# The end of a decoder kernel: seventeen stages over four token tiles, in one order for every engine

## The chip, the cores and the metric

The kernel runs on one core of one Trainium2 chip. The metric is the time of one execution on the device, in microseconds (us); the median of three runs of the kernel before is 2982.27 us (2980.43 to 2983.85). One further execution was profiled; all rows below are from it.

## The reference

2048 tokens (32 sequences of 64) of 512 features pass through three residual blocks, each on a layer-normalised input:

```python
x = x + mamba(_layernorm(x))        # in_proj, causal conv of 4 taps, silu, chunked scan with 128 heads,
                                    # gate, RMS norm over 8 groups of 1024, out_proj
x = x + attention(_layernorm(x), ctx, ctx, mask)   # 32 query heads of 16, 8 key/value heads, over 64 context rows
x = x + lora_moe(_layernorm(x))     # 4 experts of rank 16, top 2, softmax gates
```

In the attention, per sequence: `scores = q k / 4 + mask`, `probs = softmax(scores)`, `out = probs v`. In the last block: `logits = x Wr`, the two largest of four are kept and go through a softmax, `mid = x A`, `delta = sum over experts of gate * (mid B)`. The change leaves all of this as it is. The RMS norm divides each group's output by the root of its mean square; its sum of squares over the 8 chunks of a group is what the first moved piece of work computes.

## The kernel before

**The loop.** The tokens are cut into 4 blocks (`tb`) of 512, and the first block of layers into 8 groups (`g`); that gives 32 iterations (`ITERS`) of `body(tb, g)`. One iteration has 8 chunks (`CPG`). For each chunk TensorE computes the projections (`unit`, 12 matmuls of 128x512), the scan (`heads`) and the output projection (`project`, 12 matmuls into the four banks `p_out[0..3]`, one for each of the block's four tiles of 128 tokens). VectorE does the convolution, the gating (`gated`) and the sums; ScalarE the silu, the squares (`square`) and the copies `g_hi`; GpSimd the remainders `g_lo` (`g_low`), the running sum of squares (`sum_squares`) and the decays. The order of each engine's instructions is written out by hand in its own block of the program, and the engines meet only in semaphores. Weights come from rings in SBUF (`w_ring`, `o_ring`) that the SyncE queue refills.

**The tiles in the loop.** The attention and the expert layer of a finished tile of 128 tokens are spread over the next block's iterations: tile `t` opens in an even `g` (`opening`) and closes in the odd one after it (`closing`), in slots between the chunks, in the buffers `loop_tile`. 12 tiles go that way (`LOOP_TILES`). In the closing iteration GpSimd subtracts the maxima (`shifted`), ScalarE takes the exponential (`soft_exp`); VectorE has found the maxima at the end of the opening one (`maxima`).

**The end of the last iteration.** After the loop TensorE does `heads(6)`, `project(5)`, `project(6)`, `mean_squares` (4 matmuls of the summed squares `ss` with a column of ones, which the trace shows as 8 instructions) and `project(7)`. GpSimd adds the last two chunks' squares to `ss` before it makes the last remainder, so `mean_squares` waits for ScalarE and for two additions on GpSimd. VectorE then runs `accumulate`: once all four `p_out` banks are done (`out_done`), it adds them, times the inverse root `rms`, to the four tiles in `acb`, one after the other (line 1217), and counts `acc_done` once.

**The tail.** Then follow the attention and the experts of the last four tiles (`q` 0 to 3, buffers `tail_tiles[q]`) and the last five stages of tile 11, which the loop has left (`LATE`). One tile has 14 stages:

- 0: moments (VectorE, lines 1275 to 1277) and inverse deviation (GpSimd, line 1512)
- 1: the context transposed, keys and values masked (GpSimd, lines 1519 and 1521), the row normalised (`query`, line 1282), transposed (line 582) and copied to SBUF
- 2, 3: scores of each half of the heads (16 matmul instructions each) and their scaling with the mask (`scored`, line 1289)
- 4: maxima (line 1296) and their subtraction (GpSimd, line 1527), over all 2048 columns; 5: exponential
- 6, 7: sums and reciprocals (lines 1301 and 1302), probabilities transposed by halves (line 609, 8 instructions each) and copied
- 8: values (64 matmul instructions), `attended` (line 1308), `residual` (line 1319) with moments
- 9: `expert_row` (line 1326), transposed (line 628) and copied; 10: `low_rank`
- 11: `logits` and `experts` (lines 1332 to 1352); 12: `gated`, a transpose; 13: `delta` (2 matmul instructions of 512 columns) and `result` (line 1359). The tile's store follows.

`waves(stage)` sets the order, the same on each engine: wave `w` issues stage `w - q` of tile `q`, so each tile is one whole stage behind the one ahead of it, and 17 waves make up the tail. Each engine takes its instructions strictly in this order; one that waits holds up all behind it. The tiles' PSUM banks are `p_in` (q 0), `p_out[0], p_out[1]` (q 1), `p_out[2], p_out[3]` (q 2) and `p_y` (q 3). The four tiles' contexts are loaded once the last `project` is done. In SBUF, `tail_tiles` lie over the buffers of the loop.

## Time and profile before

| | us |
|---|---|
| median of 3 runs | 2982.27 |
| lowest and highest | 2980.43, 2983.85 |
| the profiled execution | 2982.17 |
| its span, first to last instruction | 2980.4 |
| last matmul of the loop's own iterations ends | 2867.15 |
| first accumulate (line 1217) starts | 2880.59 |
| last result (line 1359) ends | 2977.92 |

The span ends with the landing of the last store. "Idle before" in a row is the time for which the engine had nothing to do ahead of that group, and the name behind the arrow is what it waited for. PEclk is the granted TensorE clock as a share of its full 2.4 GHz; it stands at one of two levels, 1.00 (2.4 GHz) or 0.50 (1.2 GHz), and a value between them is a stretch that holds both. In a timeline, a group's duration covers all its instructions, and the next group's start may lie a little before its end. All numbers in these rows are of the one profiled execution.

### The profile page before, as it was taken

Reading aid. Unit: us, or ns where it says so; the run is one execution under the profiler, and the core shown is the slowest. Engines: PE = TensorE matmul, PEld = TensorE weight load, DVE = VectorE, ACT = ScalarE, POOL = GpSimd, SP = SyncE. Lnnn points to the kernel's source line nnn. Section 1 sums busy time; section 2 is a strip of 40 time slices with the busy share of each in tenths; the row PEclk is TensorE's granted clock in tenths of the full one; section 3 lists DMA queues with packets and bytes.
Section 4 is the critical chain, followed back from the end, with each engine's and each line's share of the span. In section 5 each row is a group of like instructions: output and inputs, shape, how many; then the busy total and the mean of one; then the engine's idle time right before and its main releaser. Section 6 shows DMA issues by size and latency. Waiting matters only on the chain.

```text
span 2980.4 us, 56255 instructions
## 1 busy us (share of the span) xinstructions
PE 2861.6 (96%) x22224; PEld 2292.7 (77%) x22224; DVE 2031.6 (68%) x3144; ACT 1454.3 (49%) x2168; POOL 1279.9 (43%) x820
## 2 busy tenths in 40 slices
PE   4899999999999999999999999999999999999986
PEld 3777777777878888787888878878887888888764
DVE  6677776886666766777666666677666666666656
ACT  3555556555443554445444454544544445454422
POOL 3466666676343334424324343423433342433332
PEclk8999999999999999999999999999999999999986
DMA  6777777877655555655655655555665555565510
GB/s 191 255 256 254 251 264 240 283 238 246 216 186 190 184 181 177 197 165 189 198 192 179 198 183 181 179 180 174 194 198 183 178 187 192 180 191 179 186 51 15
DMA packets 179268, 578.26 MB, mean 194 GB/s; under 512 B 25217, under 2 KB 31873, under 8 KB 170817
## 3 DMA queue, kind: packets, MB, share of 16 engines
q1 hardware_dynamic: 179008, 574.66, 58.8%
q8 instruction: 180, 2.95, 0.4%
q14 instruction: 80, 0.65, 0.1%
HBM read 460.29 MB, written 114.29 MB: 193 GB/s over the span
## 4 chain that ended last, share of the span: by engine, by line
PE 85%; DVE 9%; ACT 2%; issue 2%; POOL 1%; DMA 0%; DVEq 0%; SPq 0%; ACTq 0%; POOLq 0%
PE p_in L430 49%; PE p_out L430 22%; PE p_y L430 9%; PE p_in L509 4%; DVE cv L1157 2%; DVE o_ring L1101 1%; DVE t_y L1193 1%; PE p_y L609 1%; DVE decay L1170 1%; POOL ss L1503 0%; ACT cv L776 0%; POOL decay L1535 0%; DVE cum L1121 0%; DVE sc L1289 0%; ACT w_ring L776 0%
## 5 line engine op out<-in xcount | busy, mean ns | idle before, releaser
L430 PE MATMUL p_in<-xnb,w_ring 128*128 128x512 f32 x6912 | 1706.8, 400 | 25.5 <-DVE cv L1157 20.7
L430 PEld LDWEIGHTS p_in<-xnb,w_ring 128*128 128x128 f32 x6912 | 1278.3, 190 | 300.5 <-issue 26.1
L1157 DVE SCALAR_TENSOR_TENSOR cv<-p_in,cpar,cv 128x504 f32<-128x504 f32 (+2 forms) x960 | 704.4, 734 | 515.2 <-ACT cv L776 491.6
L1492 POOL TENSOR_TENSOR g_lo<-g_f,g_hi 128x512 fp32r<-128x512 f32 x256 | 333.6, 1303 | 1338.0 <-ACT g_hi L776 1338.0
L430 PE MATMUL p_out<-o_ring,g_hi 128*128 128x512 f32 x2048 | 648.9, 398 | 1.5 <-POOL g_lo L1492 1.5
L776 ACT ACTIVATE cv<-p_in,cpar 128x512 f32<-128x512 f32 x320 | 248.1, 775 | 696.4 <-PE p_in L430 620.7
L430 PEld LDWEIGHTS p_out<-o_ring,g_hi 128*128 128x128 f32 x2048 | 379.3, 188 | 89.7 <-issue 1.9
L430 PE MATMUL p_out<-o_ring,g_lo 128*128 128x512 f32 x1024 | 404.5, 395 | 0.0
L1181 DVE TENSOR_TENSOR x_tok<-p_in,dts 128x512 f32<-128x512 f32 x256 | 176.6, 690 | 294.4 <-PE p_in L509 292.7
L776 ACT ACTIVATE x_t<-cv 128x512 f32<-128x512 f32 x256 | 160.8, 628 | 341.9 <-DVE t_y L1193 317.0
L1503 POOL TENSOR_TENSOR ss<-ss,g_sq 128x512 f32<-128x512 f32 x192 | 312.1, 1625 | 7.5
L1484 POOL TENSOR_TENSOR w_ring<-raw_w,w_ring 128x512 fp32r<-128x512 f32 x144 | 216.7, 1529 | 76.4 <-ACT w_ring L776 76.4
L1535 POOL TENSOR_TENSOR decay<-decay,cumk 128x2048 f32<-128x2048 f32 x64 | 239.5, 3741 | 6.1 <-DMA decay<-cum_scr 4.3
L776 ACT ACT_TABLE_LOAD x183 | 234.8, 1283 | 4.0 <-PEq L1671 0.7
L776 ACT ACTIVATE sg<-p_in 128x512 f32<-128x512 f32 x256 | 150.5, 588 | 176.6 <-PE p_in L430 176.6
L430 PEld LDWEIGHTS p_out<-o_ring,g_lo 128*128 128x128 f32 x1024 | 192.1, 188 | 46.8
L1193 DVE SCALAR_TENSOR_TENSOR t_y<-x_t,dpar,p_y 128x256 f32<-128x256 f32 x512 | 210.8, 474 | 1.3 <-PE p_y L430 1.3
L509 PE MATMUL p_in<-id_sb,x_t 128*128 128x128 f32 x1024 | 157.6, 277 | 28.8 <-ACT sg L776 19.1
L509 PEld LDWEIGHTS p_in<-id_sb,x_t 128*128 128x128 f32 x1024 | 118.6, 141 | 73.9 <-DVE t_y L1193 24.0
L430 PEld LDWEIGHTS p_y<-decay,x_tok 64*64 64x64 f32 x8192 | 132.0, 135 | 55.2 <-issue 55.2
L776 ACT ACTIVATE g_hi<-g_f 128x512 fp32r<-128x512 f32 x256 | 160.2, 626 | 26.5 <-DVE g_f L1205 25.9
L1205 DVE TENSOR_TENSOR g_f<-t_y,sg 128x512 f32<-128x512 f32 x256 | 164.5, 684 | 0.0
(234 smaller groups left out, 2238.5 us busy)
## 6 DMA issues: line engine op xcount, KB each, us to landing
w_ring<-ws_scr SPq DMA_DIRECT2D x432, 512.0 KB, 3.5
o_ring<-ows_scr SPq DMA_DIRECT2D x192, 512.0 KB, 5.2
ws_scr<-w_ring SPq DMA_DIRECT2D x144, 512.0 KB, 4.9
decay<-cum_scr SPq DMA_DIRECT2D x128, 512.0 KB, 6.7
raw_w<-wt SPq DMA_DIRECT2D x144, 256.0 KB, 4.1
ows_scr<-o_ring SPq DMA_DIRECT2D x64, 512.0 KB, 6.1
raw_o<-owt SPq DMA_DIRECT2D x64, 256.5 KB, 5.5
acb<-x SPq DMA_DIRECT2D x3, 1024.0 KB, 6.2
```

The lines of the kernel that those rows point to most:

```text
L430: return nc.tensor.matmul(o, lhsT=l, rhs=r, start=first, stop=last)
L509: ins = nc.tensor.transpose(p_in[1][:, q * P:(q + 1) * P], x_t[:, c % 2, q * P:(q + 1) * P], id_sb[:, :])
L609: ins = nc.tensor.transpose(banks[rl][:, gp * P:(gp + 1) * P], pv, id_sb[:, :])
L776: return nc.scalar.activation(dst, src, func, **kw)
L1157: ins = V.scalar_tensor_tensor(acc[:, :, t:SEQ], src[:, :, 0:SEQ - t], cpar[:, 5 * m + 3 - t:5 * m + 4 - t], acc[:, :, t:SEQ], ALU.mult, A ...
L1181: V.tensor_tensor(x_tok[:, c % 2, :, :].rearrange("p q (h d) -> p q h d", h=2), p_in[1][:, :].rearrange("p (q h d) -> p q h d", q=QT, h=2) ...
L1193: ins = V.scalar_tensor_tensor(t_y[:, c % 2, :].rearrange(by_seq, q=QT, s=2)[:, s], x_t[:, c % 2, :].rearrange(by_seq, q=QT, s=2)[:, s], d ...
L1205: V.tensor_tensor(g_f[:, c % 2, :], t_y[:, c % 2, :], sg[:, (CPG * n + c) % GATES, :], ALU.mult).then_inc(g_done, 1)
L1484: T(w_ring[:, k % RING_W, 1, :, :].rearrange("p k c -> p (k c)"), raw_w[:, (UNITS * g + k) % RAW_W, :], w_ring[:, k % RING_W, 0, :, :].rea ...
L1492: T(g_lo[:, c % 2, :], g_f[:, c % 2, :], g_hi[:, c % 2, :].bitcast(F32), ALU.subtract).then_inc(glo_done, 1)
L1503: T(ss[:, :], a, g_sq[:, c % 2, :], ALU.add).then_inc(ss_done, 1)
L1535: T(decay[:, blk, :, :, :], decay[:, blk, :, :, :], last.unsqueeze(3).broadcast_to([P, 8, QT, SEQ]), ALU.subtract) \
```

## The change

- The tail's order is no longer by waves. Each of 17 stages has a position (`STAGE_AT`), each tile is 7 positions behind the one ahead, and all engines take the 68 pieces in the order of their positions. Early on that is: stage 0 of all four tiles, stage 1 of all four, stage 2 of all four, then both halves of the scores of the four tiles interleaved.
- The 17 stages are the 14 with some cut in two: the context's transposition comes apart from the row's, and the softmax is done by halves: maxima, subtraction, exponential and transposition of each half of the heads on their own semaphores. This holds for the 12 tiles in the loop too, whose two halves follow directly upon each other.
- `accumulate` is cut by tile for the last iteration: TensorE signals after each tile's three matmuls of the last chunk (`part_done`), and VectorE adds that tile and takes its moments before the next.
- The last mean squares: GpSimd no longer adds the last two chunks' squares; TensorE multiplies `ss` and both squares by the column of ones, 12 matmuls for 4.
- The last stages of tile 11 are taken out of the waves and put between the last pieces of the loop's end: its row and its transposition beside `project(5)`, `low_rank` ahead of `project(6)`, `logits` and `experts` behind it, `gated` and `delta` behind the last `project`, its `result` behind the moments of the second tile.
- The banks of the tiles are permuted (q 1 in `p_y`, q 2 and 3 in `p_out`). `o_ring` moves to the loop's part of SBUF, so that only the fourth tile's buffers lie over what the last projection reads; the contexts are loaded from the last gate on, the fourth's after the last square and the last `g_lo`.

```diff
--- before.py
+++ after.py
@@ -77,7 +77,6 @@
         main = ExitStack()
         sb = alloc(main)
         w_ring = sb("w_ring", [P, RING_W, 2, KT, P], F32R)
-        o_ring = sb("o_ring", [P, RING_O, 2, HID], F32R)
         par_all = sb("par_all", [P, GROUPS, PARAMS])
         dtk = sb("dtk", [P, 2, QT, HEADS])
         cumk = sb("cumk", [P, 2, QT, HEADS])
@@ -97,6 +96,7 @@
         sg = sb("sg", [P, GATES, TB])
         t_y = sb("t_y", [P, 2, TB])
         g_f = sb("g_f", [P, 2, TB])
+        o_ring = sb("o_ring", [P, RING_O, 2, HID], F32R)
         g_hi = sb("g_hi", [P, 2, TB], F32R)
         g_lo = sb("g_lo", [P, 2, TB], F32R)
         g_sq = sb("g_sq", [P, 2, TB])
...
@@ -222,18 +225,15 @@
             return t - 1 if t is not None and t >= 1 else None
 
         LOOP_TILES = QT * (NTB - 1)
-        STAGES, LATE = 14, 9
+        STAGE_AT, TILE_STEP = (0, 50, 72, 96, 100, 105, 114, 113, 127, 137, 153, 171, 184, 192, 204, 214, 243), 7
 
         def waves(stage):
 
-            for w in range(STAGES + QT - 1):
-                if LATE + w < STAGES:
-                    stage(LATE + w, LOOP_TILES - 1, loop_tile, p_y[:, 0, :], p_y[:, 1, :])
-                for q in range(QT):
-                    if 0 <= w - q < STAGES:
-                        y0, y1 = ((p_in[0][:, :], p_in[1][:, :]), (p_out[0][:, :], p_out[1][:, :]),
-                                  (p_out[2][:, :], p_out[3][:, :]), (p_y[:, 0, :], p_y[:, 1, :]))[q]
-                        stage(w - q, LOOP_TILES + q, tail_tiles[q], y0, y1)
+            turns = [(at + TILE_STEP * q, q, k) for q in range(QT) for k, at in enumerate(STAGE_AT)]
+            for _, q, k in sorted(turns):
+                y0, y1 = ((p_in[0][:, :], p_in[1][:, :]), (p_y[:, 0, :], p_y[:, 1, :]),
+                          (p_out[0][:, :], p_out[1][:, :]), (p_out[2][:, :], p_out[3][:, :]))[q]
+                stage(k, q, LOOP_TILES + q, tail_tiles[q], y0, y1)
 
         def ahead(g, v):
...
@@ -415,8 +415,11 @@
                 load_decay(0, 0, blk)
             iterations(sp, body)
             sp.wait_ge(y_done, CPG * ITERS)
-            sp.wait_ge(out_done, CPG * ITERS)
+            sp.wait_ge(gate_done, CPG * ITERS)
             for q in range(QT):
+                if q == 3:
+                    sp.wait_ge(sq_done, CPG * ITERS)
+                    sp.wait_ge(glo_done, CPG * ITERS)
                 load_context(LOOP_TILES + q, tail_tiles[q], tail_in[q])
             store_tile(LOOP_TILES - 1, loop_tile)
             for q in range(QT):
...
 
-                pe.wait_ge(pexp_done, t + 1)
-                if half == 1:
-                    pe.wait_ge(ptc_done, 2 * t + 1)
+                pe.wait_ge(pexp_done[half], t + 1)
+                if half == 0:
+                    pe.wait_ge(sc_done[1], t + 1)
+                else:
+                    pe.wait_ge(ptc_done[0], t + 1)
...
             iterations(pe, body)
             heads(CPG - 2, NTB - 1, GROUPS - 1, ITERS - 1)
             project(CPG - 3, NTB - 1, ITERS - 1)
+            y0 = p_y[:, 0, :]
+            pe.wait_ge(yread, CPG * ITERS)
+            experts_in(LOOP_TILES - 1, loop_tile, y0)
+
+            pe.wait_ge(ss_done, SUMS * ITERS - 2)
+            pe.wait_ge(sq_done, CPG * ITERS)
+            pe.sem_inc(hold, 1)
+            for h in range(QT):
+                tok = slice(h * P, (h + 1) * P)
+                mm(p_y[:, 1, h:h + 1], ss[:, tok], ones[:, :], True, False)
+                mm(p_y[:, 1, h:h + 1], g_sq[:, 0, tok], ones[:, :], False, False)
+                ins = mm(p_y[:, 1, h:h + 1], g_sq[:, 1, tok], ones[:, :], False, True)
+            ins.then_inc(ms_done, 1)
+            low_rank(LOOP_TILES - 1, loop_tile, y0)
             project(CPG - 2, NTB - 1, ITERS - 1)
-            mean_squares(ITERS - 1)
-            project(CPG - 1, NTB - 1, ITERS - 1)
-
-            def stage(k, t, S, y0, y1):
-
-                q = t - LOOP_TILES
+
+            c = CPG - 1
+            pe.wait_ge(o_ld[c % RING_O], 16 * ((CPG // RING_O) * (ITERS - 1 - GROUPS) + c // RING_O + 1))
+            pe.wait_ge(glo_done, CPG * ITERS)
+            for h in range(QT):
+                tok = slice(h * P, (h + 1) * P)
+                for j, (ga, wo) in enumerate(((g_hi, 0), (g_hi, 1), (g_lo, 0))):
+                    ins = mm(p_out[h][:, :], ga[:, c % 2, tok], o_ring[:, c % RING_O, wo, :], False, j == 2)
+                ins.then_inc(part_done, 1)
+            gated(LOOP_TILES - 1, loop_tile, y0)
+            delta(LOOP_TILES - 1, loop_tile, y0)
+
+            def stage(k, q, t, S, y0, y1):
+
                 if k == 1:
                     pe.wait_ge(tail_in[q], 48)
-                    if q in (1, 2):
-                        pe.wait_ge(acc_done, ITERS)
-                    if q == 3:
+                    if q == 1:
                         pe.wait_ge(yo_done, LOOP_TILES)
-                    attention_in(t, S, y0, y1)
-                if k in (2, 3):
-                    scores(t, S, k - 2, (y0, y1))
-                if k in (6, 7):
-                    probs(t, S, k - 6, (y0, y1))
-                if k == 8:
+                    if q in (2, 3):
+                        pe.wait_ge(sum_done, 2 * q - 2)
+                    context_in(t, S, y1)
+                if k == 2:
+                    rows_in(t, S, y0)
+                if k in (3, 5):
+                    scores(t, S, k // 4, (y0, y1))
+                if k in (7, 8):
+                    probs(t, S, k - 7, (y0, y1))
+                if k == 9:
                     values(t, S, y0)
-                if k == 9:
+                if k == 12:
                     experts_in(t, S, y0)
-                if k == 10:
+                if k == 13:
                     low_rank(t, S, y0)
-                if k == 12:
+                if k == 15:
                     gated(t, S, y0)
-                if k == 13:
+                if k == 16:
                     delta(t, S, y0)
 
...
-            def soft_exp(t, S):
-                act.wait_ge(sub_done, t + 1)
-                v = S.sc[:, :, :, :, :].rearrange("p h j g t -> p (h j g t)")
-                copy(v, v, ACT.Exp).then_inc(pexp_done, 1)
+            def soft_exp(t, S, half):
+                act.wait_ge(sub_done[half], t + 1)
+                v = S.sc[:, half, :, :, :].rearrange("p j g t -> p (j g t)")
+                copy(v, v, ACT.Exp).then_inc(pexp_done[half], 1)
...
+            features(LOOP_TILES - 1, loop_tile, p_y[:, 0, :])
+            middle(LOOP_TILES - 1, loop_tile, p_y[:, 0, :])
+            gate_exp(LOOP_TILES - 1, loop_tile)
+            middle_by_rank(LOOP_TILES - 1, loop_tile, p_y[:, 0, :])
...
-            def maxima(t, S):
-
-                dve.wait_ge(sc_done, 2 * t + 2)
-                V.tensor_reduce(S.mx[:, :], S.sc[:, :, :, :, :].rearrange("p h j g t -> p (h j g) t"), AX.X, ALU.max).then_inc(mx_done, 1)
+                ins.then_inc(sc_done[half], 1)
+
+            def maxima(t, S, half):
+
+                dve.wait_ge(sc_done[half], t + 1)
+                part = REP * KV // 2
+                V.tensor_reduce(S.mx[:, half * part:(half + 1) * part], S.sc[:, half, :, :, :].rearrange("p j g t -> p (j g) t"),
+                                AX.X, ALU.max).then_inc(mx_done[half], 1)
...
+            expert_row(LOOP_TILES - 1, loop_tile)
             skipped(CPG - 2, ITERS - 1)
             skipped(CPG - 1, ITERS - 1)
             gated(CPG - 2, ITERS - 1)
             gated(CPG - 1, ITERS - 1)
             variance(ITERS - 1)
-            accumulate(NTB - 1, ITERS - 1)
-
-
-            def stage(k, t, S, y0, y1):
-
-                q = t - LOOP_TILES
-                x1 = acb[:, (NTB - 1) % 2, q, :] if q >= 0 else None
+            logits(LOOP_TILES - 1, loop_tile)
+            experts(LOOP_TILES - 1, loop_tile)
+
+            def accumulate_tile(q):
+
+                if q == 0:
+                    dve.wait_ge(out_done, CPG * ITERS - 1)
+                    dve.wait_ge(rms_done, ITERS)
+                dve.wait_ge(part_done, q + 1)
+                x1 = acb[:, (NTB - 1) % 2, q, :]
+                V.scalar_tensor_tensor(x1, p_out[q][:, :], rms[:, q:q + 1], x1, ALU.mult, ALU.add).then_inc(sum_done, 1)
+
+            def stage(k, q, t, S, y0, y1):
+
+                x1 = acb[:, (NTB - 1) % 2, q, :]
                 if k == 0:
-                    dve.wait_ge(acc_done, ITERS)
+                    accumulate_tile(q)
+                    dve.wait_ge(sum_done, q + 1)
                     moments_of(S, x1).then_inc(var1_done, 1)
-                if k == 1:
+                    if q == 1:
+                        result(LOOP_TILES - 1, loop_tile, p_y[:, 0, :])
+                if k == 2:
                     query(t, S, x1)
-                if k in (2, 3):
-                    scored(t, S, k - 2, (y0, y1))
-                if k == 4:
-                    maxima(t, S)
-                if k == 6:
+                if k in (3, 5):
+                    scored(t, S, k // 4, (y0, y1))
+                if k in (4, 6):
+                    maxima(t, S, k // 2 - 2)
+                if k == 10:
                     sums(t, S)
-                if k == 8:
+                if k == 11:
                     attended(t, S, y0)
                     residual(t, S, x1)
-                if k == 9:
+                if k == 12:
                     expert_row(t, S)
-                if k == 11:
+                if k == 14:
                     logits(t, S)
+                if k == 15:
                     experts(t, S)
-                if k == 13:
+                if k == 16:
                     result(t, S, y0)
 
...
+            def shifted(t, S, half):
+
+                pool.wait_ge(mx_done[half], t + 1)
+                v, part = S.sc[:, half, :, :, :].rearrange("p j g t -> p (j g) t"), REP * KV // 2
+                T(v, v, S.mx[:, half * part:(half + 1) * part].unsqueeze(2).broadcast_to([P, part, SEQ]), ALU.subtract).then_inc(sub_done[half], 1)
...
             g_low(CPG - 2, ITERS - 1)
-            sum_squares(CPG - 2, ITERS - 1)
-            sum_squares(CPG - 1, ITERS - 1)
             g_low(CPG - 1, ITERS - 1)
             inverse_rms(ITERS - 1)
...
+                if k in (4, 6):
+                    shifted(t, S, k // 2 - 2)
+                if k == 11:
                     deviation_of(t, S, var2_done, rstd2_done)
 
...
```

## Rows read from the trace of the kernel before

**Rows 1.** The page: the span.

```profile
span 2980.4 us, 56255 instructions
```

**Rows 2.** A whole stretch: its length, busy us of each engine, clock, DMA share, GB/s.

```profile
2500.00:2867.15 367.15, 367.15 (x2959) 295.69 (x2957) 237.01 (x385) 172.69 (x252) 133.17 (x86) 1.00 0.53 172
```

**Rows 3.** Stretches of the tail, the same columns.

```profile
2920.00:2940.00 20.00, 8.48 (x119) 7.40 (x117) 14.94 (x19) 6.47 (x7) 7.78 (x3) 0.66 0.01 1
...
2960.00:2981.00 21.00, 13.09 (x29) 5.71 (x28) 10.23 (x43) 2.37 (x9) 0.54 (x1) 0.50 0.13 50
```

**Rows 4.** Timeline of VectorE: start, us, engine, line, what, [idle before].

```profile
2880.59 2.73 DVE L1217 SCALAR_TENSOR_TENSOR acb<-p_out,rms,acb 128x512 f32<-128x512 f32 x4 [2.96 <-PE p_out L430]
...
2883.68 0.68 DVE L1275 BATCH_NORM_STATS2 st<-acb 128x6 f32<-128x512 f32 x1
...
2908.01 1.67 DVE L1282 TENSOR_SCALAR row<-acb,mv,rd 128x512 f32<-128x512 f32 x1
...
2939.63 0.88 DVE L1308 TENSOR_TENSOR row<-p_out,rs 128x128 f32<-128x128 f32 x4 [4.78 <-PE p_out L430]
...
2951.85 0.15 DVE L1332 TENSOR_REDUCE lmax<-mid 128x1 f32<-128x4 f32 x1
...
2953.66 0.28 DVE L1352 SCALAR_TENSOR_TENSOR midg<-mid,gsum,gates 128x64 f32<-128x64 f32 x1
...
2977.23 0.69 DVE L1359 SCALAR_TENSOR_TENSOR x2s<-p_y,x2s 128x512 f32<-128x512 f32 x1 [2.18 <-PE p_y L430]
```

**Rows 5.** Durations of the four tiles' softmax pieces: ns min/median/max.

```profile
L1289 DVE SCALAR_TENSOR_TENSOR sc<-p_out,am x8: 678/679/691, 2897.3 to 2913.4; 128x512 f32<-128x512 f32 x8
...
L1296 DVE TENSOR_REDUCE mx<-sc x4: 2272/2280/2286, 2903.4 to 2924.0; 128x32 f32<-128x2048 f32 x4
L1527 POOL TENSOR_TENSOR sc<-sc,mx x4: 3617/3619/3621, 2905.8 to 2926.4; 128x2048 f32<-128x2048 f32 x4
L776 ACT ACTIVATE sc<-sc x4: 1902/1910/1915, 2911.4 to 2930.0; 128x2048 f32<-128x2048 f32 x4
...
L1301 DVE TENSOR_REDUCE sm<-sc x4: 2273/2275/2276, 2915.2 to 2942.3; 128x32 f32<-128x2048 f32 x4
```

**Rows 6.** Durations of the residual and of the expert row, the same columns.

```profile
L1319 DVE TENSOR_TENSOR x2s<-row,acb x4: 691/692/3420, 2927.1 to 2960.1; 128x512 f32<-128x512 f32 x4
...
L1326 DVE TENSOR_SCALAR row<-x2s,mv,rd x4: 539/542/545, 2934.3 to 2963.9; 128x512 f32<-128x512 f32 x4
```

**Rows 7.** Timeline of TensorE, end of the last iteration.

```profile
2867.98 1.16 PE L430 MATMUL p_y<-decay,x_tok 64*64 64x64 f32 x64 [0.83 <-issue]
...
2873.61 0.70 PE L430 MATMUL p_out<-o_ring,g_hi 128*128 128x512 f32 x2 [1.49 <-POOL g_lo L1492]
...
2876.48 0.95 PE L430 MATMUL p_y<-ones,ss 128*128 128x1 f32 x8
```

**Rows 8.** Timeline of ScalarE: the last two squares.

```profile
2872.03 1.13 ACT L776 ACTIVATE g_sq<-g_f 128x512 f32<-128x512 f32 x2
```

**Rows 9.** Timeline of GpSimd: the last remainder.

```profile
2876.03 1.28 POOL L1492 TENSOR_TENSOR g_lo<-g_f,g_hi 128x512 fp32r<-128x512 f32 x1
```

**Rows 10.** Timeline of TensorE in the tail.

```profile
2910.78 1.99 PE L430 MATMUL p_out<-kbd,col 64*64 64x256 f32 x16
...
2934.91 1.12 PE L628 MATMUL p_in<-id_sb,row 128*128 128x128 f32 x4 [7.56 <-DVE row L1326]
2935.95 3.63 PE L430 MATMUL p_out<-v,p_t 128*64 128x32 f32 x64
...
2941.28 1.91 PE L609 MATMUL p_y<-id_sb,sc 128*128 128x128 f32 x8
...
2967.73 1.82 PE L430 MATMUL p_y<-wa,col 128*128 128x68 f32 x8
...
2975.12 2.07 PE L430 MATMUL p_y<-wb,m_t 64*128 64x512 f32 x2 [0.36 <-ACT m_t L776]
```

**Rows 11.** A short stretch, columns as in rows 2.

```profile
2944.00:2946.00 2.00, 0.69 (x7) 0.56 (x6) 1.46 (x3) 0.54 (x2) 0.00 (x0) 1.00 0.00 0
```

83 lines of the change are left out of this document (44 added, 39 removed).

## The prediction

> **What bounds the kernel now.** I read the page for the span, then the table of stretches, then the timelines of the end. The span is 2980.4 us [rows 1]; the execution took 2982.17, so 1.8 us lie around it, and it stands 0.1 us from the median 2982.27. In the loop TensorE is busy for all of 367.15 us at clock 1.00, the others for 65% or less [rows 2]: there only TensorE's time counts, and the change removes none of it. The tail is different. In two stretches of it VectorE is busy 14.94 and 10.23 us of 20 and 21, TensorE 8.48 and 13.09, at a mean clock of 0.66 and 0.50 [rows 3]. No engine bounds it: VectorE waits for TensorE (2.96, 4.78, 2.18 us in the rows of [rows 4]), TensorE for VectorE, since each tile is a whole stage behind the one ahead. VectorE's work on one tile, by [rows 4 to 6]: accumulate 2.73/4 = 0.7; moments (0.68, and 0.4 in two short ones) 1.1; row 0.5; four scalings of 0.63 (0.68 less the overlap) 2.5; maxima 2.2; sums and reciprocals 2.6; attended 0.9; residual 0.7 with moments 1.1; expert row 0.5; logits and experts (2951.85 to 2953.94) 2.1 to 2.2; result 0.7. That is 15.6, for four tiles 62, with tile 11's pieces 65 us. From the first accumulate (2880.59) to the last result (2977.92) it is 97.3 [rows 4]. So some 32 us are idle time, and those the new order can get at.
>
> **The change, step by step.** I take each engine's new instructions in their order, start each when the engine and what it waits for are ready, and give it the duration of its row.
>
> *End of the last iteration.* The heads end at 2869.14, `project(5)` at 2872.1 (the row after it starts at 2873.61 after 1.49 idle) [rows 7]. New behind it: tile 11's four transposes, 0.6 at the full clock (half of the 1.12 in [rows 10]), to 2872.7. The mean squares no longer wait for GpSimd but for the squares, ready at 2873.16 [rows 8]. 8 instructions took 0.95 [rows 7]; 24 cost 2.85 if none overlaps more, 0.95 if the added ones hide wholly; I take 0.1 each, 2.4, nearest to the row: to 2875.6. `low_rank` 0.9 (half of 1.82, [rows 10]), to 2876.5. `project(6)` 2.9 (2873.61 to 2876.48), to 2879.4, and the first tile of `project(7)` 0.7, to 2880.1. Its `g_lo` is no wait: behind both additions it ended at 2877.3 [rows 9], and it now comes ahead of where they stood. So the edit in the queue gives 1.5 us of idle back and spends 3.9 of work, all of tile 11's; the first accumulate starts at 2880.1 against 2880.59. VectorE's share (logits, experts, `rms`) fits into its wait up to there; if it did not, the experts' 2.1 us would stand before the first accumulate. The expert row is issued while VectorE would wait for the heads.
>
> *Accumulate and moments.* Four times 1.8 is 7.2. Between them stands tile 11's result, 0.7, which waits for a transpose, a copy and a delta behind `project(7)`: 2882.2 + 0.2 + 0.3 + 1.0 = 2883.7, just when VectorE gets there. All moments are done at 2888.2 and the first row at 2888.7. Before, the fourth tile's row came at 2909.7 [rows 4]; the first tile's is late by about 2.7 us.
>
> *First scores.* TensorE has little since 2883.7 and I expect the lower clock, as [rows 3] has it here. Four transpositions of rows come before any score: 4 x 1.12, then 1.99 for a half's scores [rows 10]: 2888.7 + 6.5 = 2895.2. VectorE idles for 4 us beside its other three rows (their 0.5 can grow to 1.67 beside GpSimd, [rows 4]; the 4 us hide it).
>
> *Eight half softmaxes.* VectorE: 1.26 for two scalings and half of the maxima. A half costs between 1.14 (half of 2.28) and 2.28 [rows 5]; I take 1.17, since 512 columns cost VectorE 0.68 in a scaling and 2048 cost 2.28, nearly in proportion. 8 x 2.43 = 19.4, to 2914.6, if the others keep up. GpSimd's half: 1.8 to 2.1 (half of 3.62; with the slope between 512 columns at 1.28, [rows 9], and 2048 at 3.62), 15 to 17 in all. ScalarE: 1.05 for an exponential and 1.08 for copies, 17. TensorE: at the lower clock scores 1.99 and transposition 1.91 [rows 10], 31; at the full clock half of it, a little over 1 each, 17. So at the full clock VectorE bounds, at the lower TensorE. After some 5 us of unbroken work the clock came back before, so I take it from about 2896.
>
> *Sums, values, residual.* 4 x 2.6 = 10.4, to 2925.0; 4 x (0.9 + 0.7 + 1.1) = 10.9, to 2935.9; 4 expert rows of 0.5, to 2937.9. The values (2.0 each, or 3.63 at the lower clock) run beside the sums. The 3.42 us of one residual [rows 6] lay beside a whole subtraction on GpSimd; now the last subtraction is over before the first residual, so it costs 0.7.
>
> *Experts.* Work of 64 narrow instructions did not keep the clock up (3.63, [rows 10]), so I take the lower one here. The second tile's logits stand behind two transpositions (1.1 each) and a `low_rank` (1.8): VectorE waits 2.8 in two pieces, to 2940.7. Logits and experts 4 x 2.2 = 8.8, to 2949.5.
>
> *Delta.* By its position the first `delta` stands behind the last `gated`. So four of 2.04 (2.07 less overlap, [rows 10]) follow in a row, after 0.4 for the last transpose, and 0.7 for the last result: 2958.8 at the lower clock. I take off 1.3 for a clock that comes back within these 8 us: 2957.5. Left to the end: the store, 2.5 (2977.92 to 2980.4), and the 1.8 around the span.
>
> *What the walk misses.* Over the kernel before, with its clock, the same walk ends at 2976.4; the trace says 2977.92. I add 1.5. Sum: 2957.5 + 1.5 + 2.5 + 1.8 = 2963.3.
>
> *Edits at nothing.* The contexts' twelve loads move from 2880.6 to 2869.2 and later on SyncE's queue, whose only other work is tile 11's store; they are ready before 2884, and without that they cost what they did before. `o_ring` only moves in SBUF. In the loop each closing tile has two subtractions, exponentials and maxima for one: GpSimd +0.0 to 0.5 us, ScalarE +0.0 to 0.2, VectorE +0.0 to 0.3. The three have at least 35% idle [rows 2], so I take 0; if all of it reached TensorE it would be 12 x 1.0 = 12 us.
>
> *A page against this.* In the last 16 transpositions of probabilities (the second 8 took 1.91, [rows 10]) TensorE was at the lower clock, and right behind them the clock was 1.00 [rows 11]. The Trainium skill, page "TensorE: Matmul & The Clock Gate", section "Part 4: PE-mode transpose", says that transposes do not count as busy for the full clock. By that rule half of the softmax's work would not lift it, and rival B would be the case. The trace does not bear the rule out: those 16, behind the values, were what ran just before the clock rose.
>
> **Rivals.**
> A, the full clock from 2896 to the end. For it: TensorE's pieces follow more densely than in [rows 3]. Against: 64-instruction values and waits for VectorE. It takes off the 2.8 before the logits but 0.2, and 4 of the 8.2 for the deltas: walk 2952.7, time 2958.5.
> B, the lower clock throughout. For it: the mean of 0.50 in the last stretch [rows 3]. TensorE then bounds: per tile 1.1 + 3.9 + 3.9 + 3.6 = 12.5, from 2888.7 to 2938.6 for four; transpositions and `low_rank` to 2949.5, the last experts behind them to 2954.5, and 0.4 + 8.2 + 0.7: 2963.8, time 2969.6.
> C, the hand-written order stalls. A half goes round scores, scaling, maxima, subtraction, exponential, transposition, copy: 2.0 + 1.3 + 1.2 + 1.8 + 1.05 + 1.9 + 1.1 = 10.3 us, and its transposition stands between other halves' scores; TensorE waiting for it holds them up. With two halves in flight a half takes 5.2 us, not 2.43: +22, time 2985, no change.
> D, the same with fewer in flight, the slower side: from 5.6 us per half on (1.8 in flight) it is slower than 2988; at 1.5 in flight 6.9 us, +36, 2999. Against both: four pieces of scores lie between a half's scores and its transposition, about 4.1 us at the full clock, and the way round from its scaling is 4.2.
>
> **Numbers.** Forecast 52%, A 20%, B 20%, C 5%, D 3%. The predicted time is 2963. The forecast's own range is 2959 to 2967. The range for 8 in 10 takes in A and B, the mean squares (-1.5 to +0.5) and part of what the loop may add: 2953 to 2973. A change of 0.2%, 6 us, is about what a measurement of this kernel can tell from none. Faster by more: the forecast, A and B, 92%; within: C, 5%; slower: D, 3%.
>
> **What would show it.** First accumulate near 2880, fourth moments near 2888, first scaling near 2895. VectorE without idle time from there for 40 us; if it idles there and TensorE does not, at clock 0.5, it is B; if both idle, C or D. Four deltas in a row at the end. The residual at 0.7 four times. Clock 1.00 between 2898 and 2915. In the loop, the time at which the last iteration's heads start should be within 1 us of 2867.98; if it is later by several, the halves cost in the loop. Wrong altogether if VectorE's share of the tail is under 75%.

## The result, and the profile after

| us | before | after | after, forecast |
|---|---|---|---|
| median (lowest to highest) | 2981.35 (2977.69 to 2983.85) | 2943.55 (2943.25 to 2945.91) | 2963 (2953 to 2973) |
| span of the profiled execution | 2980.4 | 2941.2 | 2961.5 |
| last iteration's heads start | 2867.98 [rows 7] | 2850.01 | 2867.98 |
| from there to the end of the span | 112.4 | 91.2 | 93.5 |
| first accumulate to end of last result | 97.3 [rows 4] | 74.5 | 77.4, and 1.5 added |

The ratio of the medians is 0.9877, with a 95% interval of 0.9862 to 0.9892. The time lies 9.5 us below the range. Of the 39.2 us between the two spans 21.2 come from the tail, where the forecast had 18.9. The other 18.0 come from the loop, of which the forecast said that its end would move by less than 1 us.

The page of after, as [rows 1]:

```profile
span 2941.2 us, 56351 instructions
```

*The loop.* The groups of TensorE between 1500 and 2500 us, with shapes, count, busy us and mean ns of one; first before, then after:

```profile
L430 PE MATMUL p_in<-xnb,w_ring 128*128 128x512 f32 x2460 | 602.3, 397 | 0.0
L430 PE MATMUL p_out<-o_ring,g_hi 128*128 128x512 f32 x732 | 231.9, 398 | 0.0
L430 PE MATMUL p_out<-o_ring,g_lo 128*128 128x512 f32 x366 | 144.5, 395 | 0.0
```

```profile
L433 PE MATMUL p_in<-xnb,w_ring 128*128 128x512 f32 x2472 | 604.7, 397 | 0.0
L433 PE MATMUL p_out<-o_ring,g_hi 128*128 128x512 f32 x735 | 229.2, 393 | 0.0
L433 PE MATMUL p_out<-o_ring,g_lo 128*128 128x512 f32 x368 | 143.7, 390 | 0.0
```

The same matmul of the projection, at clock 1.00 in both, is 5 ns shorter where it multiplies `o_ring`, and no shorter where it multiplies `w_ring`. Matmuls overlap, so what counts is the time from one start to the next: over all after 1200 us the mean is 232.99 ns before and 227.72 after for `o_ring`, 229.64 and 229.50 for `w_ring`. An iteration has 96 of them on `o_ring`; 96 x 5.3 ns is 0.5 us, and steady iterations went from 86.95 and 87.25 us (even and odd) to 86.52 and 86.65.

Two iterations, those with the softplus of the steps, gained more: 88.94 to 86.32 us in the first. VectorE there, before and after:

```profile
1257.76 1.75 DVE L1117 TENSOR_TENSOR d_s<-d_e,cum 128x512 f32<-128x512 f32 x1
...
1261.26 3.80 DVE L1119 TENSOR_SCALAR cum<-d_e 128x512 f32<-128x512 f32 x1
```

```profile
1252.50 0.68 DVE L1159 TENSOR_TENSOR d_s<-d_e,cum 128x512 f32<-128x512 f32 x1
...
1254.93 1.40 DVE L1161 TENSOR_SCALAR cum<-d_e 128x512 f32<-128x512 f32 x1
```

And GpSimd at the same time, before and after:

```profile
1256.31 2.66 POOL L1503 TENSOR_TENSOR ss<-ss,g_sq 128x512 f32<-128x512 f32 x2
...
1260.64 4.14 POOL L1535 TENSOR_TENSOR decay<-decay,cumk 128x2048 f32<-128x2048 f32 x1
```

```profile
1251.13 3.21 POOL L1562 TENSOR_TENSOR ss<-ss,g_sq 128x512 f32<-128x512 f32 x2
1254.31 1.74 POOL L1551 TENSOR_TENSOR g_lo<-g_f,g_hi 128x512 fp32r<-128x512 f32 x1
1256.01 3.88 POOL L1594 TENSOR_TENSOR decay<-decay,cumk 128x2048 f32<-128x2048 f32 x1
```

In both traces the scaling of `cum` starts 0.6 us behind an instruction of GpSimd and ends 0.28 us behind that instruction's end. Before, it is the long subtraction (1260.64 to 1264.78), and the scaling takes 3.80 us; after, it is the remainder `g_lo` (1254.31 to 1256.05), and it takes 1.40. The 0.28 us hold in all fourteen traces. What puts the scaling one GpSimd instruction earlier is `d_s`, two instructions ahead of it: before, it starts 0.1 us behind the second addition of `ss` (1257.67 by the trace) and takes 1.75 us; after, both start at 1252.50, `d_s` takes 0.68 and the addition 1.85, where it took 1.30. No instruction here was edited; the shorter projections changed who comes first. The Trainium skill says of it (page "SBUF — State Buffer", section "Who interferes with whom") that VectorE and GpSimd share one pair of ports under "an exclusive lock", and that where a VectorE instruction needs that pair (a two-port mode, or two inputs in SBUF while GpSimd reads SBUF), the one that issues second waits for the whole of the first. By that rule, the trace agrees: the scaling ends 0.28 us behind GpSimd's instruction, whether that took 4.14 us or 1.74.

*The end of the last iteration.* Timeline of TensorE, after:

```profile
2850.01 1.16 PE L433 MATMUL p_y<-decay,x_tok 64*64 64x64 f32 x64 [0.83 <-issue]
...
2853.99 0.60 PE L637 MATMUL p_y<-id_sb,row_l 128*128 128x128 f32 x4
2855.30 0.35 PE L433 MATMUL p_y<-ones,ss 128*128 128x1 f32 x2 [0.71 <-issue]
...
2857.97 1.09 PE L433 MATMUL p_y<-wa,col_l 128*128 128x68 f32 x8
2858.86 0.84 PE L433 MATMUL p_out<-o_ring,g_hi 128*128 128x512 f32 x2
...
2860.78 0.63 PE L433 MATMUL p_out<-o_ring,g_lo 128*128 128x512 f32 x1
...
2863.05 0.40 PE L433 MATMUL p_out<-o_ring,g_lo 128*128 128x512 f32 x1
2863.28 0.62 PE L433 MATMUL p_out<-o_ring,g_hi 128*128 128x512 f32 x2
```

Stretches of after, columns as in [rows 2]:

```profile
2858.00:2860.00 2.00, 2.00 (x13) 1.75 (x14) 0.74 (x6) 0.89 (x2) 1.02 (x1) 0.82 0.34 89
2860.00:2862.00 2.00, 2.00 (x6) 1.57 (x5) 1.26 (x7) 0.83 (x2) 0.00 (x0) 0.50 0.12 34
...
2872.00:2874.00 2.00, 1.36 (x7) 1.36 (x8) 2.00 (x4) 0.20 (x1) 1.79 (x3) 0.50 0.00 0
2874.00:2876.00 2.00, 2.00 (x11) 1.65 (x9) 1.16 (x2) 1.49 (x3) 2.00 (x3) 0.50 0.00 0
2876.00:2878.00 2.00, 2.00 (x34) 1.09 (x32) 0.55 (x1) 0.70 (x2) 2.00 (x4) 0.91 0.00 0
```

Behind tile 11's transposes came 0.71 us without work, then the 24 narrow instructions of the mean squares and 8 of `low_rank`, and the clock fell to 0.50 (1.2 GHz) soon after `project(6)` had begun; that took 4.42 us (2858.86 to 2863.28) where the forecast had 2.9. The first accumulate comes 14.3 us behind the heads; in the kernel before it was 12.6.

*The tail.* Timeline of VectorE, after:

```profile
2864.27 0.75 DVE L1494 SCALAR_TENSOR_TENSOR acb<-p_out,rms,acb 128x512 f32<-128x512 f32 x1 [2.46 <-PE p_out L433]
...
2871.98 0.15 DVE L1320 TENSOR_SCALAR ve<-mv 128x1 f32<-128x1 f32 x1
2872.05 3.11 DVE L1325 TENSOR_SCALAR row<-acb,mv,rd 128x512 f32<-128x512 f32 x4
2877.45 1.29 DVE L1332 SCALAR_TENSOR_TENSOR sc<-p_in,am 128x512 f32<-128x512 f32 x2 [2.30 <-PE p_in L433]
2878.78 1.22 DVE L1340 TENSOR_REDUCE mx<-sc 128x16 f32<-128x1024 f32 x1
...
2893.90 2.35 DVE L1340 TENSOR_REDUCE mx<-sc 128x16 f32<-128x1024 f32 x2
2896.16 2.28 DVE L1347 TENSOR_REDUCE sm<-sc 128x32 f32<-128x2048 f32 x1
...
2916.80 0.69 DVE L1365 TENSOR_TENSOR x2s<-row,acb 128x512 f32<-128x512 f32 x1
...
2919.54 0.55 DVE L1372 TENSOR_SCALAR row<-x2s,mv,rd 128x512 f32<-128x512 f32 x1
2922.15 0.16 DVE L1378 TENSOR_REDUCE lmax<-mid 128x1 f32<-128x4 f32 x1 [2.06 <-ACT mid L809]
```

Against [rows 4] the row x4 stands where one row stood, and from 2877.45 to 2920 VectorE has next to no idle time. The residual takes 0.69 each time ([rows 6] had one of 3.42). From the first accumulate to the end of the last result, before:

```profile
2880.59:2977.92 97.33, 64.72 (x543) 45.04 (x543) 68.24 (x145) 27.02 (x49) 25.97 (x20) 0.65 0.06 20
```

The same of after, and its part with next to no idle time:

```profile
2864.27:2938.78 74.51, 53.01 (x540) 38.63 (x538) 61.78 (x137) 24.55 (x49) 27.50 (x24) 0.74 0.04 15
2877.45:2919.90 42.45, 29.19 (x452) 23.68 (x445) 41.48 (x70) 17.57 (x27) 20.61 (x16) 0.85 0.01 2
```

VectorE is busy for 61.78 us of the 74.51, 83%, where it was busy for 68.24 of 97.33. Of the 22.8 us between the two stretches 16.4 are its idle time, and 6.5 its own work, in part because tile 11's pieces now come ahead of the first accumulate. TensorE at its end, after:

```profile
2926.78 0.42 PE L650 MATMUL p_y<-id_sb,midg 128*64 128x128 f32 x1 [0.55 <-DVE midg L1398]
2928.80 0.42 PE L650 MATMUL p_out<-id_sb,midg 128*64 128x128 f32 x1 [1.60 <-DVE midg L1398]
2930.50 0.42 PE L650 MATMUL p_out<-id_sb,midg 128*64 128x128 f32 x1 [1.28 <-DVE midg L1398]
2930.86 2.07 PE L433 MATMUL p_in<-wb,m_t 64*128 64x512 f32 x2
```

The four deltas follow in a row, at the lower clock, from 2930.86 on.

### The profile page after: what moved, and what is told of

It is laid out like the page before. It is cut to its first block, busy times and chain, and to the rows that moved or that the text cites. A ratio compares the mean times of both kernels' runs of the same rounds, so it can differ in the third digit from the quotient of the medians.

```text
span 2941.2 us, 56351 instructions
## 1 busy us (share of the span) xinstructions
PE 2835.8 (96%) x22240; PEld 2288.6 (78%) x22240; DVE 2023.5 (69%) x3160; ACT 1453.2 (49%) x2184; POOL 1281.8 (44%) x834
## 4 chain that ended last, share of the span: by engine, by line
PE 85%; DVE 10%; ACT 2%; issue 2%; POOL 1%; DMA 0%; DVEq 0%; SPq 0%; ACTq 0%; POOLq 0%
PE p_in L433 49%; PE p_out L433 22%; PE p_y L433 8%; PE p_in L512 4%; DVE o_ring L1143 2%; DVE cv L1199 2%; DVE t_y L1235 1%; PE p_y L618 1%; DVE decay L1212 1%; POOL ss L1562 0%; ACT cv L809 0%; POOL decay L1594 0%; DVE cum L1163 0%; DVE x_tok L1223 0%; DVE sc L1332 0%
## 5 line engine op out<-in xcount | busy, mean ns | idle before, releaser
L433 PE MATMUL p_out<-o_ring,g_hi 128*128 128x512 f32 x2048 | 639.7, 393 | 0.0
```

The source lines that it names most:

```text
L433: return nc.tensor.matmul(o, lhsT=l, rhs=r, start=first, stop=last)
```

## The experiments

"Heads" is the start of the last iteration's heads (2867.98 before, 2850.01 after), and "tail" the time from there to the end of the span (112.4 and 91.2).

### The place of the ring

**`e1_ring_moved`**: the kernel before, with this part of the change alone.

```diff
-        o_ring = sb("o_ring", [P, RING_O, 2, HID], F32R)
...
         g_f = sb("g_f", [P, 2, TB])
+        o_ring = sb("o_ring", [P, RING_O, 2, HID], F32R)
```

> The kernel before with one edit alone: o_ring is allocated behind g_f instead of behind w_ring, as in the changed kernel. The changed kernel's loop ends 17.4 us sooner than the one before, with 0.07 us less in each projection of 12 matmuls (2.80 to 2.73). Theory R (the place of o_ring in SBUF sets how fast its matmuls stream): 2.73 us a projection, the loop shorter by 32 x 8 x 0.06 = 15 us, the tail as before: about 2966 us. Rival S (the softmax by halves in the loop shifts the engines against each other): 2.80 us a projection and 2981 us, no change.

Measured: 2965.03 us, ratio to before 0.9944 (0.9932 to 0.9957); heads at 2850.07, 0.06 us from the changed kernel's:

```profile
2850.07 1.11 PE L430 MATMUL p_y<-decay,x_tok 64*64 64x64 f32 x61 [0.83 <-issue]
```

The matmuls on `o_ring` start 227.70 ns apart, and the 3.80 us are gone. The gain of the loop is the ring's place. The six traces with the halves in the loop and the same two rates (after, e4, e5, e6, e8, e9) have their heads at 2850.01 to 2853.54, so the halves cost nothing that shows against the 3.5 us by which such traces differ.

**`e2_ring_64_bytes`**: before, with `o_ring` at its place but 64 bytes higher, and all behind it 128 higher.

```diff
+        pad_a = sb("pad_a", [P, 16])
         o_ring = sb("o_ring", [P, RING_O, 2, HID], F32R)
+        pad_b = sb("pad_b", [P, 16])
```

> The kernel before with 64 bytes per partition left free ahead of o_ring and 64 behind it, so that o_ring starts at 62112 instead of 62048 and every later buffer 128 bytes up. Theory R1 (what counts is the start modulo 128: g_hi starts at 32 of 128 in both kernels, o_ring at 96 before and at 32 after): 2.73 us a projection, about 2966 us. Rival R2 (what counts is where in SBUF the ring lies, near the rings that DMAs fill or next to g_hi): nothing moves, 2981 us.

Measured: 3000.4 us, ratio 1.0063 (1.0049 to 1.0077): slower than before. `o_ring` stays at 232.73 ns (232.99 before), and `w_ring`, which did not move, goes from 229.64 to 233.31. So it is not a buffer's own start alone that counts.

**`e3_starts_at_128`**: after, with 32 bytes ahead of `w_ring` and 64 behind `par_all`, so that all four operands start at multiples of 128.

```diff
+        pad_a = sb("pad_a", [P, 8])
         w_ring = sb("w_ring", [P, RING_W, 2, KT, P], F32R)
...
+        pad_b = sb("pad_b", [P, 16])
```

> The changed kernel with 32 bytes free ahead of w_ring and 64 behind par_all, so that w_ring, xnb, o_ring, g_hi and g_lo all start at a multiple of 128 bytes (before: w_ring at 96, the others at 32 of 128). Theory R1: w_ring and xnb, 216 matmuls an iteration, then have equal starts too and go from 229 to 227 ns: 32 x 216 x 2 ns = 14 us, 2930 us; if it is the distance from a multiple that counts and not the difference, all 312 matmuls gain more, down to 2900. Rival R2: 2943.5 us, no change.

Measured: 2967.84 us, ratio 0.9955 (0.9943 to 0.9968), 24 us slower than after; `w_ring` 232.51 ns, `o_ring` 229.65, and the 3.8 us of VectorE are back.

**`e7_w_ring_start`**: after, with `w_ring` alone 64 bytes up (`cmask`, 256 bytes, goes behind `ss`; pads of 64 and 192 bytes fill its place).

```diff
+        pad_a = sb("pad_a", [P, 16])
         w_ring = sb("w_ring", [P, RING_W, 2, KT, P], F32R)
...
-        cmask = sb("cmask", [P, SEQ])
+        pad_b = sb("pad_b", [P, 48])
```

> The changed kernel with w_ring 64 bytes up and cmask moved behind ss, xnb, o_ring, g_hi and g_lo where they were: w_ring at 37536, xnb at 72352. So far, mean start-to-start of matmuls by (moving start minus weight start) modulo 2048: 0 at starts of 32 modulo 128, 227.7 ns; 0 at starts of 0, 229.7; 64, 229.5; 960, 233.0; 896, 232.7; 192, 233.3; 128, 232.5. Now w_ring and xnb have difference 0 and starts of 32 modulo 128, as o_ring and g_hi have. Theory P (the pair's difference modulo 2048, and the start, set the rate): 227.7 ns in the projections of w_ring, 216 x 32 x 1.8 ns = 12 us less, 2931 us. Rival Q (the difference is not what counts): 229.5 ns or more, 2943.5 or more.

Measured: 2937.8 us (2937.14 to 2938.45), ratio 0.9851 (0.9837 to 0.9864), faster than both kernels; `w_ring` 228.60 ns (median 227, before 229), heads at 2843.31. It gained 5.7 us of the 12 expected: where matmuls on `w_ring` follow other work, the second to seventh of them keep means of 229 to 233 ns, and 227 comes from about the eighth on. The loop ends 6.7 us sooner; 1.3 of that are lost behind it, where the clock fell earlier in this trace (see `e5_by_waves`).

**`e8_all_64_up`**: after, with the first of those two pads alone, so that everything lies 64 bytes higher.

> The changed kernel with 64 bytes free ahead of w_ring: all rings, xnb, g_hi and g_lo 64 bytes up, every difference between them as it was (w_ring at 37536, xnb 72416, o_ring 153312, g_hi 169696). If only the differences count (theory P without the start): 227.7 and 229.5 ns as in the changed kernel, 2943.5 us. If the start modulo 128 counts too: the projections of o_ring near 229.7 ns or above, some 6 us more or beyond, 2950 us or more.

Measured: 2945.67 us (2942.47 to 2946.03), ratio 0.9874 (0.9861 to 0.9888), as after; 229.45 and 227.95 ns. Every start has moved and no rate has by more than 0.3 ns.

Over these kernels one number orders the rates: the start of the operand that passes through (`xnb`, `o_ring`) less the start of the one that is loaded (`w_ring`, `g_hi`), modulo 256 bytes. All steps inside the buffers are multiples of 256. Starts in bytes of a partition, as the compiler laid them out; ns from start to start, mean after 1200 us:

| | `xnb`, `w_ring` | diff. | ns | `o_ring`, `g_hi` | diff. | ns |
|---|---|---|---|---|---|---|
| before | 88736, 37472 | 64 | 229.6 | 62048, 169632 | -64 | 233.0 |
| after (e1 too) | 72352, 37472 | 64 | 229.5 | 153248, 169632 | 0 | 227.7 |
| e2 | 88864, 37472 | -64 | 233.3 | 62112, 169760 | 128 | 232.7 |
| e3 | 72448, 37504 | 128 | 232.5 | 153344, 169728 | 0 | 229.7 |
| e7 | 72352, 37536 | 0 | 228.6 | 153248, 169632 | 0 | 227.2 |
| e8 | 72416, 37536 | 64 | 229.5 | 153312, 169696 | 0 | 228.0 |
| e10 | 88992, 37536 | 0 | 228.7 | 62112, 169888 | 0 | 227.3 |
| e11 | 72352, 37600 | -64 | 233.3 | 153248, 169632 | 0 | 228.9 |

The last two were run to try the rule, from numbers given ahead.

**`e10_difference_zero`**: before, both rings at their old places.

```diff
+        pad_a = sb("pad_a", [P, 16])
         w_ring = sb("w_ring", [P, RING_W, 2, KT, P], F32R)
         o_ring = sb("o_ring", [P, RING_O, 2, HID], F32R)
+        pad_b = sb("pad_b", [P, 48])
```

> The kernel before, with both rings at their old places but 64 bytes up (w_ring 37,536, o_ring 62,112) and everything behind them 256 bytes up. In all ten kernels so far the rate of the matmuls goes with one number: the start of the moving operand less the start of the stationary one, modulo 256 bytes. It is 0 where a matmul starts 227 ns after the one before it, +64 at 229, 128 at 232 to 233, and -64 at 233. Here it is 0 for both kinds. Theory R (this difference decides): w_ring 227 to 229 ns, o_ring 227 to 228 ns, the two VectorE instructions of 3.8 us gone; the loop 23 us shorter than before's, time 2959. Theory P (o_ring is slow because of where it stands in the memory, in its lower part and far from what it is multiplied with): o_ring stays at 233 ns, only w_ring gains, time 2976. Theory N (the residue of the start itself decides, 32 modulo 64 being the good one): no change, 2982.

Measured: 2958.12 us (2955.16 to 2959.49), ratio 0.9916 (0.9901 to 0.9931), heads at 2843.17. The two groups between 1500 and 2500 us, ns min/median/max:

```profile
L432 PE MATMUL p_in<-xnb,w_ring x2484: 387/389/501, 1500.4 to 2499.3; 128*128 128x512 f32 x192
...
L432 PE MATMUL p_out<-o_ring,g_hi x736: 387/389/498, 1507.3 to 2495.9; 128*128 128x512 f32 x184
```

Padding of 256 bytes, with no other edit, makes the kernel before 25 us faster. Where `o_ring` stands in the memory does not matter.

**`e11_difference_minus_64`**: as e7, but pads of 128 and 128 bytes.

> The kernel after with w_ring alone 128 bytes up (37,600), so that the difference between the rows that pass through and w_ring is -64 modulo 256 where it was +64; all other starts as in e7. Theory R: w_ring 233 ns as in e2, o_ring 227 to 228 ns; the loop 20 us longer (26 if the GpSimd collisions come back with it), time 2964 to 2969. Theory P or N: w_ring stays at 229 ns and the time within 3 us of 2943.6.

Measured: 2968.83 us (2967.4 to 2971.62), ratio 0.9951 (0.9935 to 0.9968). The same view:

```profile
L435 PE MATMUL p_in<-xnb,w_ring x2456: 390/394/502, 1500.6 to 2499.8; 128*128 128x512 f32 x189
...
L435 PE MATMUL p_out<-o_ring,g_hi x724: 387/389/501, 1503.5 to 2493.6; 128*128 128x512 f32 x181
```

64 bytes between e7 and e11 are 31 us. Theories P and N both fall; the rule gave the first time to within 1 us and the second within its span (the 3.8 us of VectorE had come back).

### The tail

**`e4_squares_on_gpsimd`**: after, with the mean squares as before (GpSimd adds, 8 matmuls), behind `project(6)`.

> The changed kernel with the last mean squares as before: GpSimd adds the last two chunks' squares to the sum, and TensorE does 4 matmuls with the column of ones, behind project(6). In the changed kernel the 12 narrow matmuls ran ahead of project(6), the granted clock was 0.50 right behind them, and project(6) took 4.2 us where it took 2.9. Theory C (the narrow matmuls let the clock fall, and that costs more than the wait for GpSimd that they save): project(6) in 2.8 us, first accumulate some 2 us sooner, 2941.5 us. Rival G (the wait for GpSimd, 2.6 us longer on the way to the last remainder, costs as much as the clock gives): 2943.5. If the clock falls without them: 2945.

Measured: 2947.06 us (2943.31 to 2949.63), ratio 0.9883 (0.987 to 0.9897) against after's 0.9877: no difference. Its TensorE, and then its VectorE:

```profile
2859.04 0.71 PE L433 MATMUL p_out<-o_ring,g_hi 128*128 128x512 f32 x2
...
2861.86 0.95 PE L433 MATMUL p_y<-ones,ss 128*128 128x1 f32 x8
2862.67 0.72 PE L433 MATMUL p_out<-o_ring,g_hi 128*128 128x512 f32 x2
```

```profile
2862.85 0.16 DVE L1243 TENSOR_SCALAR msv<-p_y 128x4 f32<-128x4 f32 x1 [6.88 <-PE p_y L433]
...
2864.94 0.74 DVE L1486 SCALAR_TENSOR_TENSOR acb<-p_out,rms,acb 128x512 f32<-128x512 f32 x1
```

The clock does not fall here: `project(6)` takes 2.8 us for 4.4, and the first accumulate comes 13.05 us behind the heads for 14.26. It would come 1.5 sooner still, but tile 11's experts, issued behind the variance, fill VectorE up to it. From the heads to the end it is 90.9 us against 91.2. So this part of the change pays nothing that a run shows: what it saves in waiting it gives back in instructions and in the clock.

**`e5_by_waves`**: after, with each tile a whole stage behind the one ahead.

```diff
-        STAGE_AT, TILE_STEP = (0, 50, 72, 96, 100, 105, 114, 113, 127, 137, 153, 171, 184, 192, 204, 214, 243), 7
+        STAGE_AT, TILE_STEP = tuple(range(0, 170, 10)), 10
```

> The changed kernel with its 17 stages in waves again: STAGE_AT is 0, 10, ..., 160 and TILE_STEP 10, so each tile is one whole stage behind the one ahead of it; the halved softmax, accumulate by tile, tile 11's place and o_ring's place stay. Theory O (the order of stages is what takes the idle time out of the tail): VectorE waits again as before, the tail from the first accumulate to the last result is 15 to 22 us longer than 74.5, 2960 us or more. Rival H (halving and the earlier accumulate do it, any order would): under 5 us longer, 2948 or less.

Measured: 2963.84 us (2956.59 to 2966.95), ratio 0.9932 (0.9919 to 0.9945); tail 108.3. From the first accumulate on, columns as in [rows 2]:

```profile
2869.42:2958.71 89.29, 56.23 (x540) 37.14 (x538) 62.20 (x136) 24.40 (x49) 26.51 (x24) 0.72 0.03 13
```

The row ends at the last result's start, which is 0.7 us ahead of its end. VectorE's work is the same (62.2 us, after 61.8), and its idle time is 27 for 13. From the first accumulate to the end of the last result it is 90.0 us for 74.5: of the 22.8 that this stretch lost 15.5 are the order. The other 1.6 of the 17.1 by which e5's tail is longer lie ahead of the first accumulate, and they are no work of the order. In e5, e7 and e11 the clock fell while the matmuls of the mean squares were still running, and the first accumulate came 15.9 us behind the heads; in after, e3, e6, e8 and e12, with the same instructions there, it fell later, among those of `low_rank` or in `project(6)`, and the accumulate came at 14.3.

**`e9_accumulate_in_one`**: after, with the first accumulate waiting for all four tiles.

```diff
-                dve.wait_ge(part_done, q + 1)
+                dve.wait_ge(part_done, QT)
```

> The kernel after, but the first accumulate of the tail waits until all four tiles of the last project are done, as it was before. The four tiles take 2.7 us at the full clock, of which the first is on the path now; so the first accumulate would start 2.0 us later, at 2866.3 instead of 2864.3. Theory 1 (VectorE sets the end from there on): the end moves by nearly as much, +1.9 us, time 2945.4. Theory 2 (the rows' transposes and the first scores hide it, VectorE idles 2.3 us before its first scaling): +0, 2943.6.

Measured: 2948.14 us (2946.49 to 2948.49), ratio 0.9883 (0.9868 to 0.9897). This interval overlaps after's, so the reading rests on the trace. The first accumulate comes 2.0 us later behind the heads. The end of the span comes at 93.9 us, 2.7 later than in after and 1.8 later than in e3 and e8, which have after's tail and the first accumulate at 14.3 as after has (92.1 each). Theory 1 fits: nothing hides the accumulate.

**`e6_delta_forward`**: after, with `delta` of a tile behind `gated` of the next instead of all four behind the last.

```diff
                 if k == 15:
                     gated(t, S, y0)
+                    if q >= 1:
+                        delta(t - 1, tail_tiles[q - 1], ...)
-                if k == 16:
+                if k == 16 and q == 3:
                     delta(t, S, y0)
```

> The changed kernel with one edit on TensorE: the delta of tile q is issued behind the transpose (gated) of tile q + 1 instead of behind all four. In the changed kernel TensorE waits 1.6 and 1.3 us for the third and fourth transpose and then runs four deltas in a row, 8 us at clock 0.50. Theory D (the deltas are the last stretch's length and can fill these waits): last result 1.5 to 2 us sooner, 2941.8 us. Rival: the delta delays the next transpose by as much as it saves, 2943.5 us.

Measured: 2945.55 us (2943.7 to 2947.22), ratio 0.9876 (0.9863 to 0.989): no difference to after. Its trace: from the first accumulate to the end of the last result 72.1 us against 74.5, but its loop ended 2.8 us later, of which 2.0 were there at the second iteration; that is within the 3.5 us by which traces of one loop differ.

```profile
2930.03 2.07 PE L433 MATMUL p_in<-wb,m_t 64*128 64x512 f32 x2
2932.03 0.42 PE L650 MATMUL p_out<-id_sb,midg 128*64 128x128 f32 x1
...
2934.73 3.78 PE L433 MATMUL p_out<-wb,m_t 64*128 64x512 f32 x4
```

The deltas now lie in the 1.60 and 1.28 us that TensorE waited for `midg`.

**`e12_ring_and_delta`**: e6 and e7 together.

> The kernel after with both edits that shortened something: w_ring 64 bytes up as in e7 (-5.7 us of time) and the deltas of e6, which in its trace took 2.4 us off the way from the first accumulate to the last result (71.5 against 73.8 us between their starts), although its time stood 2.0 us above that of after because its loop began and ran 2.8 us later. If the two add up, and the late loop of e6 was chance: 2943.6 - 5.7 - 2.4 = 2935.4, and 71.5 us between those two starts again. If the late loop belongs to the edit: 2939 to 2940.

Measured: 2935.67 us (2932.92 to 2939.0), ratio 0.9846 (0.9832 to 0.9859): faster than before and after, and what was expected if e7's time and e6's shorter tail add up (2935.4). From the start of the first accumulate to that of the last result it is 71.3 us, as in e6 (71.5; after 73.8). Whether it beats e7 alone (0.9837 to 0.9864) is open: its profiled execution has the shorter tail (88.6 for 92.5, of which 1.6 are the clock) and again a later loop (heads at 2846.77 for 2843.31).

## Why the prediction was wrong

The step that failed is the one under "Edits at nothing": "`o_ring` only moves in SBUF". It was taken at 0, with no row behind it; it is worth 17 to 18 of the 20 us by which the forecast missed. Two things make it up. From the fourteenth iteration's start to the last one's the two kernels drift by 12.5 us (iteration starts 1202.83 and 1197.99, then 2780.54 and 2763.18): two iterations by 2.6 each, where VectorE's scaling no longer waits for GpSimd's long subtraction, and the other 16 by 0.46 on average. (That iteration took 88.9 to 89.5 us in the four traces with the 3.8 us and 86.0 to 86.4 in the ten without.) The 12 iterations before that gave 4.0. The argument "only TensorE's time counts, and the change removes none of it" was right in its first half: it is why 5 ns on each of 3,072 matmuls came through to the end. The step could have been given two sides: the profile before had the same shape at 229.6 ns on one ring and at 233.0 on the other, and nothing in it said why. The sign that the forecast gave for the loop, heads within 1 us of 2867.98, named only a loop that ends later; no case had it end sooner.

The steps of the tail, in us behind the heads' start (2867.98 for the forecast, 2850.01 for the trace):

| | forecast | measured |
|---|---|---|
| first accumulate starts | 12.1 | 14.3 |
| fourth moments done | 20.2 | 22.1 |
| first scaling starts | 27.2 | 27.4 |
| sums start | 46.6 | 46.2 |
| last row done | 69.9 | 70.1 |
| experts done | 81.5 | 80.4 |
| last result done | 89.5, and 1.5 added | 88.8 |

- *End of the iteration.* The edit was to spend 3.9 us and give 1.5 back, and the first accumulate to come 0.5 sooner behind the heads than before (12.6); it came 1.7 later. The 24 matmul instructions took 2.7 (forecast 2.4), TensorE idled for 0.7 ahead of them (0.5), and `project(6)` took 4.4 us for 2.9, at the lower clock, which no step had.
- *First scores.* The forecast had the lower clock for the scores and the first scaling 6.5 us behind the first row. The clock was 0.50 through the 16 transposes of rows (2872.6 to 2876.3), and 0.91 in the stretch behind them: the first scaling came 4.8 us after the transposes began. This made good what the step before had lost. Here again transposes were what ran ahead of a rising clock, at a TensorE busy for 1.36 and 2.00 of 2 us. Rival B is not borne out. Nor is the statement of the Trainium skill that the prediction sets beside it (page "TensorE: Matmul & The Clock Gate", section "Part 4: PE-mode transpose"), if these transposes are of the kind that it means, which no run shows.
- *Eight halves.* 18.7 us for 19.4; VectorE bounds them, as said. GpSimd's half took 1.90, ScalarE's 1.06, VectorE's maxima 1.21 for 1.17. The clock was not 1.00 throughout, as the signs had it: it was 0.50 from 2890 to 2892, and VectorE did not wait.
- *Sums, values, residual.* 23.9 us for 23.3, and four residuals at 0.69. The values ran at clock 1.00 (2.06 us a tile), and the clock fell in the 5.28 us without work behind them. That 64 narrow instructions do not keep the clock up was misread from [rows 10]: the piece of 3.63 us began at 0.50.
- *Experts and delta.* Waits of 2.06 and 0.35 for 2.8; then 10.4 us to the experts' end from the last row for 11.6, and 8.3 to the last result for 8.0. The lower clock that was taken here is what came, but by luck, since the reason given for it did not hold. The 1.3 taken off for a rising clock was wrong: it stayed at 0.50.
- *What the walk misses.* The 1.5 was not needed: the walk came out at 89.5 for 88.8.
- *Halves in the loop.* 0 was taken, and nothing else shows: e1 has none and ends its loop at 2850.07, the six traces with them at 2850.01 to 2853.54.
- *VectorE's idle time.* The prediction puts it at some 32 us of the 97.3 before; the trace has 29.1.
- *The rivals' sums.* A's walk adds up to 2952.2 where 2952.7 stands, and the 5.0 us of B from 2949.5 to 2954.5 have no row. The forecast rests on neither.

So in the tail the forecast case was the right one of the five, VectorE's share is 83%, and of the rivals neither A nor B nor a stall came. That the steps end within 0.7 us of the trace is luck in part, since errors of 2.2 us up to the first accumulate and of 2.0 from there to the first scaling cancel. e5, e9 and e4 price the parts: the order 15.5, the accumulates by tile about 2, the mean squares nothing. The softmax by halves and the place of tile 11's stages were not tried apart from the rest.

## What to carry to other kernels

A change that moves a buffer changes more than its lines say: read the same matmul's rate on each pair of buffers, and where two pairs differ, try the start of the operand that passes through and of the one that is loaded at the same residue modulo 256 bytes, which was the fastest here, before the loop is tuned further. Where one engine is busy for the whole of a loop, a few ns on each of its instructions add up (5.3 ns on 3,072 of them were 16 us here), so no edit that touches its operands may be priced at 0. In a tail of dependent stages the order is worth more than any single instruction that it removes.
